# Third attention: row-halved score matmuls, a scratch in DRAM laid out as it is read, and a new order of the slot

## What is computed

```python
q = (x @ Wq).reshape(b, t, 2 * H, HD).transpose(0, 2, 1, 3) * scaling
k = (x @ Wk).reshape(b, t, 2 * H, HD).transpose(0, 2, 1, 3)
v = (x @ Wv).reshape(b, t, H, 2 * HD).transpose(0, 2, 1, 3)
scores = jnp.einsum('bhqd,bhkd->bhqk', q, k)
aw = jax.nn.softmax((scores + causal).astype(jnp.float32), axis=-1)
aw = aw.reshape(b, H, 2, t, t)
aw = aw[:, :, 0] - lam * aw[:, :, 1]
attn = jnp.einsum('bhqk,bhkd->bhqd', aw, v)
attn = attn * jax.lax.rsqrt(jnp.mean(attn * attn, axis=-1, keepdims=True) + 1e-05)
attn = attn * (1.0 - LAMBDA_INIT)
return attn.transpose(0, 2, 1, 3).reshape(b, t, H * 2 * HD) @ Wo
```

## Time and profile before

| | |
|---|---|
| Median of 3 runs | 2285.53 us (2275.45 to 2287.73) |
| The profiled run | 2258.67 us, span 2256.8 us |
| PE busy | 1910.5 us, 85% |
| DVE, ACT, POOL busy | 1373.3, 762.5, 896.1 us |
| Mean granted clock of PE | 0.925 of full |
| DMA packets | 116497, of them 113676 under 2 KB |
| Stage 3 | from 643.8 us to about 1419 us of the span |

### The profile page before, as it was taken

How to read it: one execution, slowest core, us unless ns; L and a number is a source line. 1 busy time by engine, 2 the same in 40 slices (tenths; PEclk the granted TensorE clock), 3 DMA queues, 4 the chain that set the end, 5 groups by cost and what they waited for, 6 DMA issues and landing times.

```text
span 2256.8 us, 41632 instructions
## 1 busy us (share of the span) xinstructions
PE 1910.5 (85%) x13912; PEld 1418.4 (63%) x13912; DVE 1373.3 (61%) x3587; ACT 762.5 (34%) x1575; POOL 896.1 (40%) x917
## 2 busy tenths in 40 slices
PE   8999997899956887888898967798986787998887
PEld 5655554789944666566666645576765666886343
DVE  4777775565523554445445534688874676887775
ACT  2444443122212454444454534011112222443332
POOL 0354455665541344333443422133334222664333
PEclk9999998999988999899999989799999888999787
DMA  6100000100025344334433430000000100000011
GB/s 221 41 8 7 5 7 8 32 8 9 10 38 108 48 62 63 49 61 56 64 65 54 66 57 5 10 10 7 9 21 27 36 14 21 10 14 15 28 36 43
DMA packets 116497, 82.05 MB, mean 36 GB/s; under 512 B 10524, under 2 KB 113676, under 8 KB 116108
## 3 DMA queue, kind: packets, MB, share of 16 engines
q1 hardware_dynamic: 116364, 80.22, 17.6%
HBM read 62.49 MB, written 16.91 MB: 35 GB/s over the span
## 4 chain that ended last, share of the span: by engine, by line
PE 54%; SPq 16%; DVE 16%; issue 6%; DMA 4%; POOL 2%; ACT 1%; DVEq 1%; POOLq 0%; ACTq 0%
PE PS L1017 15%; SPq L2249 10%; SPq L2263 5%; DMA QS<-maxT 3%; PE PS L665 3%; PE PS L722 2%; PE PS L1172 2%; PE PS L738 2%; DVE xn L494 2%; PE PS L504 2%; PE PS L1920 2%; PE PS L719 2%; PE PS L1889 1%; PE PS L689 1%; PE PS L1942 1%
## 5 line engine op out<-in xcount | busy, mean ns | idle before, releaser
L2105 DVE TENSOR_REDUCE negmax<-PS 128x2 f32<-128x512 f32 (+1 forms) x384 | 241.3, 684 | 275.7 <-PE PS L1884 275.1
L535 POOL TENSOR_TENSOR X<-X,y_sb 128x512 f32 (+1 forms) x128 | 165.4, 1292 | 205.9 <-DVE y_sb L530 200.9
L2036 ACT ACTIVATE pw<-PS 128x512 f32<-128x512 f32 x256 | 140.1, 595 | 261.9 <-PE PS L1921 261.5
L530 DVE TENSOR_TENSOR y_sb<-PS,ga_sb 128x512 f32<-128x512 f32 x96 | 66.4, 692 | 245.5 <-PE PS L1971 71.9
L1920 PE MATMUL PS<-QS,KS 128*128 128x256 bf16 x512 | 104.8, 285 | 89.5 <-DMA QS<-maxT 89.5
L1017 PE MATMUL PS<-we_hi,h_parts 128*128 128x512 f32 x512 | 177.0, 406 | 0.0
L494 DVE TENSOR_SCALAR xn<-X,mv,rs 128x256 f32 (+1 forms) x256 | 157.7, 657 | 22.8 <-POOL rs L487 21.5
L514 ACT ACTIVATE hT<-PS,modT 128x256 f32<-128x256 f32 x256 | 130.0, 558 | 108.9 <-PE PS L504 107.8
L1017 PE MATMUL PS<-l_h_parts,lut_hi 128*128 128x256 f32 (+1 forms) x768 | 143.0, 288 | 6.7 <-POOL l_h_parts L1140 6.7
L485 POOL TENSOR_TENSOR rs<-mv,eps 128x2 f32<-128x2 f32 x128 | 26.8, 210 | 297.3 <-DVE mv L478 297.1
L1506 DVE SCALAR_TENSOR_TENSOR l_acc<-PS,rt_g,l_acc 128x256 f32<-128x256 f32 x256 | 105.9, 475 | 25.6 <-PE PS L1017 21.7
(11 more groups left out here) (270 smaller groups left out, 4806.4 us busy)
## 6 DMA issues: line engine op xcount, KB each, us to landing
ga_sb<-ga_dram SPq DMA_DIRECT2D x128, 128.0 KB, 2.9
qk_dram<-qk_parts SPq DMA_DIRECT2D x16, 768.0 KB, 4.1
QS<-qk_dram SPq DMA_DIRECT2D x192, 64.0 KB
KS<-qk_dram SPq DMA_DIRECT2D x192, 64.0 KB
wmod<-in_wmod SPq DMA_DIRECT2D x4, 1536.0 KB, 13.4
y_out<-X SPq DMA_DIRECT2D x16, 256.0 KB, 2.2
X<-in_x SPq DMA_DIRECT2D x1, 3072.0 KB, 17.1
QS<-maxT SPq DMA_DIRECT2D x192, 4.0 KB
```

What stands on the lines that cost most here:

```text
L535: pool.tensor_tensor(xb(b), xb(b), y_sb[b.par][:, :, :], ALU.add).then_inc(s.x.sem, 1)
L2036: act.activation(to.rearrange("p a n -> p (a n)"), bank(4 + n), ACT.Exp).then_inc(s.prob.sem, 1)
L2105: dve.tensor_reduce(to, src, AX.X, ALU.max, negate=True).then_inc(s.max.sem, 1)
```

## The change

Two things that belong together, and a new order for them.

**Layout.** The columns of Wq and Wk are permuted on the host so that the two maps of a head come out of the projection on different halves of the partitions. `qk_dram` now holds the stacks as they are read: for q and k and each half, six terms of 64 partitions x 1 KB. It is written by 12 transfers of 64 partitions (a part that occurs in several terms is written several times; six transfers for k as soon as k's parts are ready, six for q) and read by 4 transfers of 48 rows of 8 KB. QS loses its zero blocks and halves its size; the transfers of zeros go. The maxima go in with one transfer for each half of the rows, 2 for each half of the heads instead of 6.

**Matmuls.** A score matmul contracts over 64 partitions only (48 for the maxima), and the two maps' matmuls are issued in turns on the two halves of PE's rows, each with a PSUM bank of its own. The masks of two heads are merged into one matmul; they stay on all 128 rows. A unit is now eight (head, map) pairs: three steps (n = 0, 1, 2) of two banks each, four units per batch. `values` takes eight in one go and ACT copies their result in one instruction of 512 columns, four instead of eight.

**Order.** k, q and v projections, the transposed maxima, the norm's transposes, the output projection and the layer norm's transposes all share bank 0, each waiting until the one before is copied out. The norm and output of a batch move one slot later (batch i-2 in slot i), so the stage has one slot more. POOL splits k and q apart, 512 columns at a time; its square root for the norm moves behind the second split of maxima. The gate load of this stage moves to the end of SP's slot. The tiles of stage 2 lie at other addresses.

```diff
-        out[f"l1_w{n}"] = two(a[f"L1_attn_W{n}"])
+        w = a[f"L1_attn_W{n}"]
+        if n in "qk":
+            w = w.reshape(D, 8, KH, 2, 8).transpose(0, 2, 3, 4, 1).reshape(D, D)
+        out[f"l1_w{n}"] = two(w)
...
-    out["no_max"] = np.zeros((3, 16, T), bf)
...
-        QS, KS = wbuf("QS", [P, 16, 2, T], 2, BF16), wbuf("KS", [P, 16, T], 2, BF16)
+        QS, KS = wbuf("QS", [P, 16, T], 2, BF16), wbuf("KS", [P, 16, T], 2, BF16)
...
+
+        N_TERMS, Q_RUNS, K_RUNS = 6, ((0, 3, 0, 0), (3, 5, 1, 0), (5, 6, 2, 0)), ((0, 3, 0, 1), (3, 5, 0, 1), (5, 6, 0, 0))
+        qk_dram = nc.dram_tensor("qk_dram", (2, 2, 2, N_TERMS, P // 2, KH * T), BF16, kind="Internal").ap()
...
+            def project_q(b):
+                pe.wait_ge(*s.k(b))
+                project_T(b, "q", s.q_ps)
...
+
+
+            def half_rows(x, pr, g, a, b_, rows):
+                return x[64 * pr:64 * pr + rows, g, a:b_]
...
+            def max_pair(b, o, n):
+                u = 6 * o + 2 * n
+                q, k = QS[b.par], KS[b.par]
+                if u == 0:
                     pe.wait_ge(*stack_ready(b))
...
+                if u >= 2:
+                    pe.wait_ge(*s.max(b, u - 1))
+                elif (b - 1).ok:
+                    pe.wait_ge(*s.max(b - 1, 23))
+                banks = [bank(1 + (u + pr) % 3) for pr in range(2)]
+                if n == 0:
+                    for pr in range(2):
+                        pe.matmul(banks[pr], ident_b[:, :], later4[:, :, :], start=True, stop=False)
+                    for j in range(4):
+                        for pr in range(2):
+                            last_ = pe.matmul(banks[pr][:, j * P:(j + 1) * P], half_rows(q, pr, 4 * o + j, 0, P, M_ROW),
+                                              half_rows(k, pr, 4 * o + j, 0, P, M_ROW), start=False, stop=j == 3)
+                            if j == 3:
+                                last_.then_inc(s.max_ps.sem, 1)
+                else:
+                    for j in range(2):
+                        for pr in range(2):
+                            g = 4 * o + 2 * (n - 1) + j
+                            pe.matmul(banks[pr][:, j * T:(j + 1) * T], half_rows(q, pr, g, P, T, M_ROW),
+                                      half_rows(k, pr, g, 0, T, M_ROW), start=j == 0, stop=False)
+                    for pr in range(2):
+                        pe.matmul(banks[pr].rearrange("p (j k) -> p j k", j=2)[:, :, P:T], ident_b[:, :], later4[:, 0:2, :],
+                                  start=False, stop=True).then_inc(s.max_ps.sem, 1)
...
+            def exp_pair(b, o, n):
+                u = 6 * o + 2 * n
+                q, k = QS[b.par], KS[b.par]
+                if u >= 2:
+                    pe.wait_ge(*s.prob(b, u - 1))
+                elif (b - 1).ok:
+                    pe.wait_ge(*s.prob(b - 1, 23))
+                if u < 4 and (b - 1).ok:
+                    pe.wait_ge(*s.u(b - 1, 4 if u == 0 else 3))
+                if u % 12 == 0:
+                    pe.wait_ge(*max_ready(b, u // 12))
+                banks = [bank(4 + (u + pr) % 3) for pr in range(2)]
+                if n < 2:
+                    for j in range(2):
+                        for pr in range(2):
+                            g = 4 * o + 2 * n + j
+                            pe.matmul(banks[pr][:, j * T:(j + 1) * T], half_rows(k, pr, g, 0, P, 64),
+                                      half_rows(q, pr, g, 0, T, 64), start=j == 0, stop=False)
+                    for pr in range(2):
+                        pe.matmul(banks[pr].rearrange("p (j q) -> p j q", j=2)[:, :, 0:P], ident_b[:, :], earlier4[:, 0:2, :],
+                                  start=False, stop=True).then_inc(s.score.sem, 1)
...
+            def values(b, o):
+                pe.wait_ge(*s.prob(b, 6 * o + 6))
+                if o:
+                    pe.wait_ge(*s.oT(b, o))
...
+                for pr in range(2):
+                    for kt in range(TT):
+                        for j in range(4):
+                            v = l1_vpad[b.par][:, kt, 4 * o + j, :]
+                            to = PS[32 * j:32 * j + 32, 7, pr * T:(pr + 1) * T]
+                            if kt == 0:
+                                pe.matmul(to, v, pw[o % 2][pr][j // 2][:, j % 2, :], start=True, stop=False)
+                            else:
+                                last_ = pe.matmul(to[:, P:T], v, pz[o % 2][pr][:, j, :], start=False, stop=True)
                 last_.then_inc(s.pv.sem, 1)
...
+            def slot(i):
+                c, d, e = i + 1, i - 1, i - 2
+                if i.ok:
+                    max_pair(i, 0, 0)
+                if c.ok:
+                    project_k(c)
+                if d.ok:
+                    exp_pair(d, 2, 0)
+                    exp_pair(d, 2, 1)
+                if i.ok:
+                    max_pair(i, 0, 1)
+                if d.ok:
+                    values(d, 1)
+                    exp_pair(d, 2, 2)
+                if i.ok:
+                    max_pair(i, 0, 2)
+                if c.ok:
+                    project_q(c)
+                if d.ok:
+                    exp_pair(d, 3, 0)
+                if i.ok:
+                    max_pair(i, 1, 0)
+                if d.ok:
+                    values(d, 2)
+                    exp_pair(d, 3, 1)
+                if i.ok:
+                    max_pair(i, 1, 1)
+                if d.ok:
+                    exp_pair(d, 3, 2)
+                if i.ok:
+                    max_pair(i, 1, 2)
+                if e.ok:
+                    normed_T(e)
+                if i.ok:
+                    max_pair(i, 2, 0)
+                    max_T_first(i)
+                if d.ok:
+                    values(d, 3)
+                if i.ok:
+                    max_pair(i, 2, 1)
+                if c.ok:
+                    project_v(c)
+                if i.ok:
+                    max_pair(i, 2, 2)
+                if d.ok:
+                    by_token(d)
+                if i.ok:
+                    exp_pair(i, 0, 0)
+                    max_pair(i, 3, 0)
+                if e.ok:
+                    out(e)
+                if i.ok:
+                    for n in (1, 2):
+                        exp_pair(i, 0, n)
+                        max_pair(i, 3, n)
+                next_tokens(i)
+                if i.ok:
+                    exp_pair(i, 1, 0)
+                    values(i, 0)
+                    max_T_second(i)
+                    exp_pair(i, 1, 1)
+                    exp_pair(i, 1, 2)
+
+            slots(pe, slot, -2, LOOP2, B + 1)
 
         def l1a_scalar(act, pl, s):
...
+            def evict_qk(b, n, ps, done, scale):
+                act.wait_ge(*ps(b))
+                if (b - 1).ok:
+                    act.wait_ge(*s.split(b - 1, 1 if n else 3))
+                if (b - 2).ok:
+                    act.wait_ge(*scratch_ready(b - 2, n))
+                act.activation(qk32[:, n, :], bank(0), ACT.Copy, scale=scale)
+                act.activation(qk_parts[b.par][:, 0, n, :], bank(0), ACT.Copy, scale=scale).then_inc(done.sem, 1)
...
+            def split_qk(b, c, n):
+                hi, mid, lo = (qk_parts[b.par][:, a, c, :] for a in range(3))
+                pool.wait_ge(*(s.k if c else s.q)(b))
+                pool.tensor_tensor(qk_rest[:, c, :], qk32[:, c, :], hi, ALU.subtract).then_inc(s.split.sem, 1)
+                pool.wait_ge(*s.split(b, n + 1))
+                pool.tensor_tensor(mid, qk_rest[:, c, :], zero[:, :].broadcast_to([P, KH * T]), ALU.add).then_inc(s.split.sem, 1)
+                pool.wait_ge(*s.split(b, n + 2))
+                pool.tensor_tensor(lo, qk_rest[:, c, :], mid, ALU.subtract).then_inc(s.parts.sem, 1)
...
+            for c, runs in ((1, K_RUNS), (0, Q_RUNS)):
+                sp.wait_ge(*s.parts(b, 2 - c))
+                for r in range(2):
+                    for n0, n1, part, step in runs:
+                        src = qk_parts[b.par][64 * r:64 * r + 64, part:part + (n1 - n0 if step else 1), c, :]
+                        if not step:
+                            src = src.broadcast_to([P // 2, n1 - n0, KH * T])
+                        sp.dma_start(qk_dram[b.par, c, r, n0:n1].rearrange("n p x -> p n x"), src).then_inc(scratch_in[b.par][c], 16)
...
+            for c in (1, 0):
+                if not c or not (i - 1).ok:
+                    sp.wait_ge(*scratch_ready(i, c))
+                for r in range(2):
+                    to = (QS, KS)[c][i.par][64 * r:64 * r + M_ROW, :, :].rearrange("p g t -> p (g t)")
+                    sp.dma_start(to, qk_dram[i.par, c, r].rearrange("n (d g) x -> (n d) (g x)", d=8)).then_inc(stack_in[i.par], 16)
...
+                r0, r1 = 64 * pr + M_ROW, 24 * pr
+                sp.dma_start(QS[b.par][r0:r0 + 3, 8 * half_:8 * half_ + 8, :], maxT[half_][r1:r1 + 24, :])\
+                  .then_inc(max_in[b.par], 16)
...
-                    if i.ok:
+                    if i.ok and p != 2:
...
```

(36 more changed lines are left out.)

415 lines of the change are left out of this document (163 added, 252 removed).

## The result

| | before | after |
|---|---|---|
| Median | 2280.49 us | 2162.55 us (2155.16 to 2165.08) |
| The profiled run | 2258.67 us | 2160.2 us |
| Its span | 2256.8 us | 2158.4 us |
| Mean granted clock of PE | 0.925 | 0.934 |
| DMA packets | 116497 | 68177 |

Both medians are of four runs on one chip. The ratio is 0.9478, 95% interval 0.9433 to 0.9522: 118 us or 5.2% faster. The forecast was 2201 us, inside its range of 2125 to 2260; it was 38 us too high.

A forecast was written before the change was run, and what follows sets the result against it. Stage 3 was taken as bound by the SP queue's circle of stack and maxima transfers, period 44.3 us. Gains 18 + 6 + 15 x 4.0 = 84 us off 2258.7 give 2175; 27 carried over gives 2201, range 2125 to 2260.

The forecast's parts named there:

- A: Rival: PE-bound, shape changes overlap weight loads and waits shrink; period 36.8 us, time 2149 us; chance 0.22.
- the frame: Whole-kernel step: the 27 us between profiled run and median before carries over, turning 2175 into 2201 us.
- The queue leaves the circle: SP queue in stage 3: four reads, at most 4.4 us, replace 19.3 us between the halves' maxima; writes cost nothing.
- TensorE's work: PE's work per stage 3 slot at full clock: 33.4 us, against 35.2 in the order before.
- The change of shape: PE's cost of switching tile shape in stage 3: 0.11 us each, 47 a slot, 5.2 us; up to 9.4 at 0.2.
- They eat the whole gain of the halves: Stage 3 on PE: 5.2 us of shape changes a slot cancel the 5.3 us a batch from overlapping halves.
- The waits: PE's pauses per stage 3 slot in the new order, at exponentials, transposes, divisions, banks and maxima: 6.9 us.
- The clock: PE in stage 3: full clock throughout, as the longest wait is 1.4 us; sign: near 1.0 in every 50 us stretch.
- The start of the stage: Stage 3's filling: first max at 667, 18 us earlier, plus 6 us from the first slot's queue.
- B: Rival: shape changes cost 0.2 us or pairs only half overlap; period 43.7 us, time 2252 us; chance 0.15.
- C: Rival: slower than before, PE takes the queue's place fully; time 2344 us; chance 0.05.
- D: Rival: SP queue stays in the circle through dear writes or late maxima; period 44 us, time 2257 us; chance 0.08.

The follow-up runs named there:

- e10: Changed kernel with both maps' score matmuls on the first 64 rows, so the halves can't overlap: 2243.9 us.
- e3: Changed kernel with the masks cut into two 64-row steps on both halves, 24 changes of shape a slot instead of 47: 2166.7 us.
- e6: e1 with TensorE's loop over slots 4 to 11 of the third attention written out as straight code: 2165.0 us.
- e7: Changed kernel with TensorE's loop over slots 4 to 11 of the third attention written out as straight code: 2159.4 us.
- e8: e3 (masks in row halves) with TensorE's loop over slots 4 to 11 written out as straight code: 2136.2 us.
- e1: Kernel before with the new layout and queue transfers alone, TensorE's old order on full rows and the zero blocks kept: 2191.2 us.
- e5: Kernel before with TensorE's loop over slots 4 to 11 of the third attention written out as straight code: 2272.8 us.
- e4: Changed kernel with its four stack reads of 48 rows cut into 24 of 8 rows, each row still 8 KB: 2272.5 us.
- e12: e11 with the first transpose of the maxima moved behind the values of the last head group on TensorE: 2105.5 us.
- e11: e8 with the last head group's first pair of maxima moved ahead of the first pair of probabilities on TensorE: 2123.3 us.
- e2: Changed kernel with the two halves' score matmuls not in turns, all heads of one half first: 2160.9 us.

## Why the prediction was right, and where it was off

**The result against the forecast.** The period of 39.3 us lies in the forecast's 38.3 to 42.3. The time of 2162.6 lies below the forecast's own range of 2171 to 2231, and nearer to A's 2149 than to 2201; that it does so is mostly the 24 us of the frame (below), not the mechanism.

**The queue leaves the circle: right.** Writes issue in 0.65 us each (3.90 and 3.83 for six), between the bounds of 0.38 and 1.1. The cover was nearly used up: q's six end at 913.06 and the first maxima go at 913.38, 0.3 us later, where I had 5.0 us free less 2.3 to 6.6. Had they been dear, they would have stood on the path.

**TensorE's work: 33.4 us forecast.** From 760 to 1240 us it is busy 418.25 us of 480, so 34.3 of a slot's 39.3, the stretches at a lower clock counted at their length. In a slot at full clock (941.59 to 980.13 us) it is busy 33.53 of 38.54, so the 33.4 was right. The overlap, taken as full (5.3 us), measures 4.8 (e10). The change of shape, taken as 0.11 us, measures 0.10 (0.33 less the 0.22 of four matmuls at full overlap; 0.32 to 0.22 in e3's trace). The upper bound of 0.2 from the fp32 rows didn't apply.

**"They eat the whole gain of the halves": not what the runs show.** Two things were mixed. First, 47 is the number of changes in the new slot, not what the change adds. The kernel before has 14 in a slot of its trace, which the sum held in its 0.89 for the values; 33 come on top, 3.3 us at 0.10, against an overlap worth 4.8. The sum's own totals, 33.4 against 35.2, leave 1.8 us of TensorE's work. Second, that gain is there, and it is the new order's waits that take it. Eight slots of e6 (layout alone) and of e7 (the changed kernel), both as straight code:

```profile
878.40:1190.80 312.40, 285.44 (x3124) 220.23 (x3169) 172.54 (x345) 164.88 (x337) 138.49 (x136) 0.99 0.52 88
```

```profile
868.90:1185.50 316.60, 270.56 (x2881) 155.06 (x2912) 175.28 (x344) 159.10 (x305) 139.81 (x160) 0.97 0.45 85
```

TensorE is busy 35.7 us of a slot in e6 and 33.8 in e7, 1.9 less; it is idle 3.4 us in e6 and 5.8 in e7, 2.4 more. So the times are the same, 2165.0 and 2159.4. The two kernels differ in the halves, the merged masks and the order at once; no run has the halves in the old order. (The profiled run of e7 took 2171.8 us, 12 above its median.) That changes of shape cost what the sum says is shown by e8: with 23 fewer, TensorE is busy 31.5 us in a slot (931.0 to 968.5 us) where the changed kernel's slot at full clock has 33.5. Its time is 23 us under e7's: 1.1 us a slot against those of 38.6, 16 in all; the rest fits the clock, which stays at 1.00 behind the same pauses in e8 (912 to 917 us).
The Trainium skill, TensorEngine Tiling (Array Packing), Key Properties, has the rule that changing the tiling mode drains the engine. The traces agree that a change costs time, 0.10 us each.

**A step that was missing.** In the loop as it stands the changed kernel is 29 us under e1 all the same, and e6 gets 26 of them by straight code alone: TensorE's loop is loaded again in e1 and not in the changed kernel. Nothing in my sum had this. I had seen periods of 38 to 53 us before and averaged over them. As before's total doesn't change without these waits (e5) but e1's does (26 us), the forecast's 40.3 against 44.3 was right for a kernel whose loop isn't reloaded, and that the changed one is that was luck.

**The waits: 6.9 us forecast, about 5.0 measured.** The named places hold: 1.17 (1.3 forecast), 1.05 (1.1), 0.58 and 1.39 (0.8 and 1.4). The second half's transpose (0.3) and the landing of its maxima (0.5) don't show, and of the six small ones (1.5) those of 0.58 (at 932.98) and 0.24 do. Waits shorter by 1.9 us and TensorE busy for 0.9 longer make 39.3 instead of 40.3.

**The clock: partly wrong.** I took full speed since no pause was over 1.4 us, and named near 1.0 in every 50 us stretch as the sign. Ten of eleven have 0.97 or more, one has 0.93. Behind 0.58 + 1.26 to 1.39 us it falls in 8 of 13 slots (0.66 to 0.79 over 5 us); the seven of 40.1 us are 1.6 longer than those of 38.5, 0.8 on average: nearly all of the 0.9 above.

**The start of the stage: right.** The first pair of maxima comes at 668.9 (667 forecast), and batch 2's write 22.4 us earlier than before (24 forecast for fill and first slot).

**The sum.** 22.4 + 13 x 4.97 = 87.1 us at batch 15's write, and 98.5 between the profiled runs; the forecast was 84. The other 24 of the 38 us are the frame. I let the 27 us by which before's profiled run lay under its median carry over; in the changed kernel it is 2.4 (2162.6 and 2160.2). That was the frame's error: a profiled run is one draw from the spread. Of the 13 runs of the kernel before beside e1 to e4, eleven lie between 2251.9 and 2284.8, while the changed kernel's four lie between 2155.2 and 2165.1. e4, which waits for its stacks, spreads too (2252.5 to 2282.2 in ten runs). That the changed kernel spreads less because the circle is gone is likely, and not shown.

**The rivals.** A (36.8 us) was not this kernel, but e12 is there with 35.5: the waits did shrink once they were worked on, and its changes of shape are half as many. B and C asked for dear changes or no overlap; e10 shows that even without overlap the kernel is 1.4% faster than before, so C needed both. D's premise is e4's: there the stacks, not the maxima, come late, and the time is that of before.

## What to carry to other kernels

Relieve the queue first, then look at the array: here the layout alone brought 83 of the 118 us, and two-row tiling with a full-height mask between the pairs gave back most of its overlap in changes of shape. Read busy and idle time apart: what the halves saved in work, the new order lost in waits until e11 and e12 moved them. Keep operations of one shape together. Cut transfers so that the number of rows fills the engines, and read the DMA share over the landing, since the issue times don't tell. Where slots of a rolled loop differ by some 8 us with a period of one pass, look for waits by "issue" at its first instructions and for code loads beside them, and try the loop as straight code.

## What was unexpected of the hardware

- A jump back of TensorE's loop cost 6.3 to 6.5 us of waiting (e3), 4.6 to 4.7 in two pieces (e1), and 7.8 to 8.3 us of a slot with what follows from it, in loops of some 790 matmuls a pass (e1) and some 830 (e3). The loop of some 730 was not loaded again (no load in 230 us) and shows no such wait. Straight code was loaded all along (18 and 17 loads in 230 us) without such waits; e7 is no slower than the changed kernel.
- A change between full rows and 64-row tiles costs 0.10 us for bf16 matmuls of 64 and 48 rows. Two matmuls on one half after the other and then two on the other cost no more than turns (e2, 0.33 us with the change of shape in both).
- 24 reads of 8 rows issue in 0.34 us each, 24 of 16 rows in 0.46, four of 48 rows in 0.42. The landing, not the issue, told them apart: 2272 and 2174 us.
